# Decoder layer with attention, cross attention and routed experts: 8 of the 79 expert tiles are run between the routing steps of the last sequence, with a ring of 16 results

## The reference, cut to what matters

```python
logits = xf @ Wg.T                       # xf: 4096 tokens, Wg: 16 experts
probs = jax.nn.softmax(logits, axis=-1)
topw, topi = jax.lax.top_k(probs, K)     # K = 2
...
for e in range(E):
    h = jax.nn.silu(xf @ W1[e]) * (xf @ W3[e])
    out = out + gates[:, e:e + 1] * (h @ W2[e])
```

## Time and profile before

| what | value |
| --- | --- |
| time, median of 3 runs | 822.4 us (821.83 to 822.49) |
| the profiled execution, its own time | 823.12 us |
| its span, first to last instruction | 821.3 us |
| granted clock of TensorE, mean | 0.993 of full speed |
| PE busy | 798.6 us, 97% of the span |
| DVE busy | 598.0 us, 73% |
| ACT busy | 432.8 us, 53% |
| POOL busy | 396.8 us, 48% |

### The profile page before, as it was taken

The page is one execution under the profiler, slowest core; times in us unless marked ns, Lnnn a source line. Parts: engine busy times, 40 slices in busy tenths (PEclk is TensorE's granted clock), DMA queues, the critical chain, the costliest instruction groups (busy, mean ns, idle before and its releaser), DMA issues.

```text
span 821.3 us, 21021 instructions
## 1 busy us (share of the span) xinstructions
PE 798.6 (97%) x5949; PEld 758.3 (92%) x5950; DVE 598.0 (73%) x1722; ACT 432.8 (53%) x1185; POOL 396.8 (48%) x567
## 2 busy tenths in 40 slices
PE   9999999999999999999999999999988999999995
PEld 8898999999999999999999999999987799999994
DVE  4757777888787877878787778887675566666663
ACT  4473554637265463737355453726243267667673
POOL 3332134444534454454535444353435358787875
PEclk9999999999999999999999999999999999999997
DMA  8786573655739284564828375573499458777780
GB/s 266 256 290 233 194 256 120 244 204 193 256 125 308 81 281 161 201 242 160 280 95 309 108 254 175 187 263 127 156 425 368 146 106 134 127 132 128 131 132 2
DMA packets 105673, 161.19 MB, mean 196 GB/s; under 512 B 10672, under 2 KB 69616, under 8 KB 104752
## 3 DMA queue, kind: packets, MB, share of 16 engines
q1 hardware_dynamic: 79264, 115.33, 42.0%
q0 software_dynamic: 15792, 35.17, 17.2%
q10 hardware_dynamic: 10576, 10.19, 4.7%
HBM read 50.14 MB, written 112.47 MB: 198 GB/s over the span
## 4 chain that ended last, share of the span: by engine, by line
PE 82%; DVE 6%; ACT 6%; issue 3%; DMA 1%; SPq 1%; POOL 1%; POOLq 0%; DVEq 0%; ACTq 0%
PE ps L797 70%; PE ps L808 5%; PE ps L1037 3%; PE ps L1147 2%; PE ps L1169 2%; ACT fT_hi L1305 2%; ACT relu_v L1306 2%; ACT phi L1292 1%; DVE fT_lo L1508 1%; DVE snmax L1681 1%; DVE smax L1677 1%; DVE pr L1670 1%; DVE xn_attn L1501 0%; ACT pr L1351 0%; DVE stat L1490 0%
## 5 line engine op out<-in xcount | busy, mean ns | idle before, releaser
L788 POOL DMA_INDIRECT out<-narrow,sidx x79 | 122.4, 1549 | 46.1 <-DVE sidx L1886 20.7
L1220 ACT ACTIVATE xn3T<-ps 128x512 f32<-128x512 f32 x17 | 10.2, 597 | 138.8 <-PE ps L808 136.2
L797 PE MATMUL ps<-w_hi,fT_hi 128*128 128x256 f32 x256 | 79.8, 312 | 2.4 <-DVE fT_lo L1508 2.1
L1292 ACT ACTIVATE phi<-ps,nmax 128x128 f32<-128x128 f32 x256 | 73.4, 381 | 9.2 <-DVE nmax L1629 9.0
L1508 DVE TENSOR_TENSOR fT_lo<-relu_v,fT_hi 128x512 fp32r<-128x512 f32 x64 | 52.3, 818 | 33.2 <-ACT relu_v L1306 33.0
L797 PE MATMUL ps<-w_lo,fT_hi 128*128 128x256 f32 x256 | 72.3, 282 | 0.0
L797 PE MATMUL ps<-w_hi,fT_lo 128*128 128x256 f32 x256 | 72.2, 282 | 0.0
L1306 ACT ACTIVATE relu_v<-ps,b_sb 128x256 f32<-128x256 f32 x128 | 69.1, 540 | 0.0
L1305 ACT ACTIVATE fT_hi<-ps,b_sb 128x256 fp32r<-128x256 f32 x128 | 68.0, 531 | 1.5 <-PE ps L797 1.5
L605 POOL TENSOR_TENSOR veps<-mv,eps_ln 128x2 f32<-128x2 f32 x48 | 10.8, 225 | 118.4 <-DVE mv L1494 118.4
L797 PE MATMUL ps<-hT_hi,w_hi 128*128 128x256 f32 x256 | 67.2, 284 | 0.0
(11 more groups left out here) (300 smaller groups left out, 2744.6 us busy)
## 6 DMA issues: line engine op xcount, KB each, us to landing
expert_rows<-zero_rows SPq DMA_DIRECT2D x16, 4352.0 KB, 16.0
narrow<-expert_rows ACTq DMA_DIRECT2D x71, 136.0 KB
expert_up_hi<-X SPq DMA_DIRECT2D x16, 352.0 KB, 2.7
e_lo<-expert_up_lo POOLq DMA_DIRECT2D x2, 2816.0 KB, 12.8
e_hi<-expert_up_hi POOLq DMA_DIRECT2D x2, 2816.0 KB, 22.1
part_raw<-in_E SPq DMA_DIRECT2D x30, 176.0 KB
expert_up_lo<-part_raw SPq DMA_DIRECT2D x15, 352.0 KB, 3.1
X<-in_x SPq DMA_DIRECT2D x16, 256.0 KB
```

The costliest lines, as they stand in the source:

```text
L788: pool.indirect_dma_start(out_rows, bass.IndirectOffsetOnAxis(sidx[:, u:u + 1], 0), yg[:, u, :], None, bounds_check=NT * P - 1, oob_is_err ...
L797: return pe.matmul(out_, lhsT, rhs, start=start, stop=stop)
L1220: return act.activation(out_, in_, ACT.Copy)
L1292: last = act.activation(phi[:, g, h, :], ps[:, g, h * M:(h + 1) * M], ACT.Exp, bias=nmax[:, g, h:h + 1])
```

## The change

- The plan of the first 8 tiles (`EARLY`) is made from the counts of the first 13 sequences (`EARLY_SEQS`): for each expert in turn, its tiles that are already full (`early_count`, `early_sum`, `early_tiles` on DVE, in the last turns). SP loads their rows in the last turn (`load_early`).
- The last turn (`NSEQ + 2`) is gone. The norm, router, choice, count, placing and storing of the last sequence stand between the pieces of slots 0 to 2; the plan of the other tiles (`late_count`, `late_sum`, `late_tiles`) in slots 1 and 2; loading of tiles 8 to 13 in ACT's slot 6 (`load_late`). The filler behind the last cross attention and ahead of the first tile is gone.
- The other tiles leave out what the first 8 took (`taken`).
- `yg` and `sidx` are rings of 16 (`RING`): slot s writes them when scatter s-16 has landed. The rows `xg` stay a ring of 8.
- Scatters among the first 8 tiles wait for the one or two before them whenever the experts differ (`early_waits`), without a test of tokens; tile 8 always waits for tile 7 and 6, tile 9 for tile 7 (the `ALU.max`). From tile 8 the test of meeting tiles is made from both sides. POOL's edge gathers stand behind scatter 1, and the edges are read in slots 9 to 11.
- The expert weights are loaded by SP in pieces, 14 of 16 experts of the low up parts already in turn 15, and `e2a` and `e2b` by POOL at other places of its turn.
- The gate's exponential of the last sequence moves from ACT to POOL, as a power of e.

```diff
+    EARLY = 8
+    RING = 2 * GB
+    EARLY_SEQS = NSEQ - 3
...
+            def early_waits():
+                dve.wait_ge(early_plan, EARLY_TILES)
+                for k in range(1, ADDING):
+                    last = dve.tensor_tensor(other_early[:, k - 1, k:], expert_i[:, k:EARLY], expert_i[:, 0:EARLY - k],
+                                             ALU.not_equal)
+                then(last)
+                for k in range(1, ADDING):
+                    last = dve.scalar_tensor_tensor(added_need[:, k - 1, k:EARLY], other_early[:, k - 1, k:], 16.0,
+                                                    round_of[:, 0:EARLY - k], ALU.mult, ALU.add)
+                last.then_inc(early_plan, 1)
...
+                for k in range(1, ADDING):
+                    last = dve.tensor_tensor(other_expert[:, k - 1, k:], lasts[:, 0:SLOT_TILES - k], firsts[:, k:], ALU.is_ge)
+                then(last)
+                for k in range(1, ADDING):
+                    last = dve.tensor_tensor(meeting[:, k - 1, k:], meeting[:, k - 1, k:], other_expert[:, k - 1, k:],
+                                             ALU.mult)
+                then(last)
+                for k in range(1, ADDING):
+                    last = dve.tensor_scalar(meeting[:, k - 1, EARLY:EARLY + k], meeting[:, k - 1, EARLY:EARLY + k], 1.0, None,
+                                             ALU.max)
...
             def scatter_index(s, u):
-                if not (isinstance(s, int) and s < GB):
-                    hold(dve, scattered[u], (s - u) * PER + 16)
-                dve.tensor_scalar(sidx[:, u:u + 1], xg[:, u, D:D + 1], float(NT * P), None, ALU.add)\
+                if not (isinstance(s, int) and s < RING):
+                    hold(dve, scattered[u % GB], rounds(s, u) - 16)
+                dve.tensor_scalar(sidx[:, u:u + 1], xg[:, u % GB, D:D + 1], float(NT * P), None, ALU.add)\
...
+                if first(s):
+                    place_own(NSEQ - 1, 5)
+                    dve.wait_ge(egap_ready, NSEQ)
+                    gates(NSEQ - 1)
+                if isinstance(s, int) and s == 1:
+                    late_count()
+                    late_sum()
+                if isinstance(s, int) and s == 2:
+                    late_tiles()
...
+            def load_late():
+
+                act.wait_ge(plan_ready, 1)
+                tiles = [tile_of(s) for s in range(EARLY, EARLY + 2)]
+                act.wait_ge(placed, NSEQ * 16 * TOPK * TS)
+                for s in range(EARLY, 2 * EARLY - 2):
+                    load_rows(s, s, tiles[s - EARLY] if s - EARLY < len(tiles) else tile_of(s))
```

More of the change, by code:

```diff
@@ L597, in _ @@
             pool.wait_ge(const_ready, N_CONST - 2)
-            for whole, short in ((before, before_01), (ones, ones_01)):
-                pool.tensor_copy(short[:, :], whole[:, :]).then_inc(const_ready, 1)
+            for whole, short in ((before, before_01), (ones[:, :], ones_01)):
+                pool.tensor_copy(short[:, :], whole).then_inc(const_ready, 1)
             pool.wait_ge(const_ready, N_CONST)
@@ L720, in turn @@
                         split_ctx(b + 1)
-                if r is not None and not last_turn:
+                if r is not None:
                     keep_rows(r)
@@ L1100, in turn @@
                     ffn_out(1, FC - 2, FC).then_inc(w2_ps, 1)
-                if b is not None and not last_ffn:
+                if b is not None and not last_ffn and not last_cross:
                     router(b, 6)
@@ L1283, in turn @@
                     round_part(*splits_of(i))
-                def own_rows(kept):
-                    for j in range(TOPK):
-                        last = copy(kept[:, :, j, 0:D], xn3)
-                    last.then_inc(rows_kept, 1)
                 def features(g):
@@ L1379, in turn @@
                     round_part(splits_of(i)[0])
-                if r is not None and not last_ffn and not last_cross and not last_turn:
+                if r is not None and not last_ffn and not last_cross:
                     choice_counts(r)
@@ L1613, in logits_in, with choice_seen, summed @@
                     .then_inc(logit_ready, 1)
+            def choice_seen(r):
+                hold(dve, chosen, (r + 1) * CHOICE_STEPS)
+                dve.tensor_tensor(oh[:, :, :], hot[:, 0], hot[:, 1], ALU.add).then_inc(oh_ready, 1)
+                if not first(r):
+                    dve.wait_ge(egap_ready, r)
+                dve.tensor_tensor(gap[:, :], best[:, :, 1], best[:, :, 0], ALU.subtract)\
+                    .then_inc(gap_ready, 1)
+            def summed(counted):
+                cum, cbufs, n = counted, (cum_a, cum_b), 1
+                while n < NE:
+                    dst = cbufs[0]
+                    cbufs = cbufs[::-1]
+                    dve.tensor_copy(dst[:, 0:n], cum[:, 0:n])
+                    then(dve.tensor_tensor(dst[:, n:], cum[:, n:], cum[:, 0:NE - n], ALU.add))
+                    cum, n = dst, 2 * n
+                return cum
@@ L1767, in turn @@
                         part_rest(p, n)
-                if b is not None:
+                if b is not None and not last_cross:
                     if not first(b):
```

508 lines of the change are left out of this document (316 added, 192 removed).

## The result

The changed kernel takes 837.12 us (median of 4 runs, 834.24 to 839.49), the kernel before beside it on the same chip 822.44 us: a ratio of 1.0175 (95% interval 1.0141 to 1.0209). It is slower by 14.7 us; the forecast was 832.6, with a range of 825 to 840. The profiled execution has a span of 834.6 us and took 836.78.

A forecast was written before the change was run, and what follows sets the result against it. PE bounds the kernel before, POOL's scatter chain the changed one: start 644.9, plus 58.7, 95.1 and 25.9, puts the last scatter at 824.6; 6.9 more gives a span of 831.5, a median of 832.6 us, range 825 to 840.

The forecast's parts named there:

- Nine neighbour waits, 5.0 us a trip: POOL, scatters 0 to 15: nine wait for the direct neighbour, 5.0 us each; with gathers 58.7 us against 36.5 before.
- Scatter 0 at 644.9: POOL, behind the last sequence's stores: first scatter starts at 644.9 instead of 654.87, 10 us sooner; range 643.5 to 648.
- Weights and early rows, nothing: DMA loads ahead of tile 0: weights arrive in time, early row loads lie under the last cross attention; 0 to 1 us.
- Steps 15 to 64, 95.1 us, and the last 14, 25.9: POOL's later scatters: its own pace as before for 95.1 us, then 14 steps at 1.85 us, 25.9, ending at 824.6.
- The end: After the last scatter: the span ends 6.9 us behind its start at 824.6, giving 831.5 us.
- PE's side, slot 7 at 658.5: PE, first eight slots moved into the 21 us stretch: slot 7 ends near 658.5 instead of 665.5, a 7.0 us gain.
- the faster rival: Short trips let scatters catch PE, whose 7.0 us gain shows: 815.4 us, or up to 822; chance 0.09.
- The ring: The ring of 16 lets PE run ahead but does not make POOL faster; PE loses a us or two near slot 30.
- No change: PE's new waits or half clock in slots 0 to 7 cancel its gain and POOL isn't late: 822.4 us; chance 0.05.

The follow-up runs named there:

- e2: Kernel before with neighbour waits forced at the nine tiles where the changed kernel has them, nothing else changed: 846.72 us, ratio 1.0239.
- e7: Changed kernel with the results of tiles 0 to 14 written nowhere and no waits among those scatters: 828.71 us, ratio 1.0082.
- e0: Changed kernel run again unaltered, on the chip of a later call, for comparison: 837.58 us, ratio 1.020.
- e4: Changed kernel without the 2048 KB load of the low down weights, the high part used instead: 833.07 us, ratio 1.0133.
- e5: Changed kernel with ACT's row loads of tiles 8 to 13 issued two each in slots 5, 6 and 7: 838.24 us, ratio 1.0195.
- e3: Changed kernel with `sidx` waiting for scatter s-8 instead of s-16, `yg` still a ring of 16: 839.06 us, ratio 1.0126.
- e8: Changed kernel with crowded experts first, tiles 8 to 13 loaded in three places, low down weights loaded later, edges tested earlier: 823.95 us, ratio 0.9993.
- e9: The changed kernel with the repairs of e8 but the old order of experts, so nine neighbour waits stay: 836.75 us, ratio 1.014.

## Why the prediction was right, point by point, and what it mis-sized

The direction, the bound and the mechanism came out as forecast. The size is 4.5 us too small: one term is 5.2 too small, and all others together are 0.7 too large.

- **Nine neighbour waits, 5.0 us a trip.** Right in number and place. The nine steps sum to 43.2 us, 4.80 each. Seven of them lie between 4.61 and 4.88, the one at tile 3 takes 5.80, the one at tile 14 3.79. With the gathers, steps 0 to 15 take 57.0 where 58.7 was written: -1.7. e2 shows that the waits alone are enough. One thing the sum leaves out stayed hidden by luck: scatter 8 also waits for the test's numbers, which come in slot 11. By e7 they would hold it to 682.44 without any of the first five waits, 0.9 us before it started.
- **Scatter 0 at 644.9.** This term failed. It starts at 650.07, 5.2 late and 2 beyond the upper bound (648.94 and 4.0 in e0, the same kernel again). The step that went wrong is "Weights and early rows, nothing": the prediction let the loads of the early rows lie under the last cross attention and never asked what else was in the DMA engines when they were issued. They stood behind the down weights `e2b` and `e2a_lo`, landed 6.6 and 9.6 us after their issue where that is known, and left PE idle for 4.3 us and then at 1.2 GHz, ahead of the last sequence's router. The prediction's reading that the DMA engines are full until about 638 was the kernel before's, and it held here until 632. e4 takes 2 MB away and gets scatter 0 at 645.16 and 833.07 us. The low clock itself had been named, but only for the rival in which it cancels the gain.
- **Steps 15 to 64, 95.1 us, and the last 14, 25.9.** Right: 94.9 and 25.9. POOL's 1.85 us set the pace to the end.
- **The end.** 6.7 us behind the last scatter, 6.9 written. +5.2 - 1.7 - 0.2 - 0.2 gives a span of 834.6 for 831.5. The other 1.4 us of the median are what lies around the span (2.2 against 1.8) and that the median is 0.3 above the profiled execution, not 0.7 below.
- **PE's side, slot 7 at 658.5.** Wrong by 10.5 us: it ends at 669.05, 3.5 after the 665.5 of before. The row of small waits had been listed, but not the first hole, nor that ACT issues six loads (4.96 us in the timeline) before it splits tile 8's rows, nor the half clock in both. The second hole did not reach the time, since PE isn't the bound there (e5); the first did, through scatter 0. Had the waits been cheap, all of it would have counted: e7 is the faster rival put to the test, and it takes 828.7, not 815.4.
- **The ring.** That it only lets PE run on is right within 2.5 us (e3).
- **The rivals.** "Faster" needed trips of 3.9 us. One of nine was shorter. The rule weighed there, of the Trainium skill ("DMA: Bandwidth & Descriptors", section "Anatomy of one DMA — SWDGE (gpsimd) path"), gives an estimate of 2.3 us for a transfer of this size; the landing of L844 is 2.7, 3.9 and 4.5, so the trace doesn't agree. "No change" had the half clock on PE right and POOL wrong.

So the loss has two layers. POOL's chain is the outer one, and by e7 8.9 us can be had by taking its waits away. Then PE is the bound, 5.2 us late at its last result. Of the two holes the first is worth more: by tile 71's result from the mark, its repair brings PE 4.7 to 5.4 us (e4 against e0 and the changed kernel), that of the second 2.9 to 3.6 (e5), and with both e8 is 3.7 ahead of the kernel before, for 7.0 forecast at slot 7.

## What to carry to other kernels

An engine that sits off the bound at 1.85 us of 2.00 has no room: count the waits that a new order puts into its chain before counting what the new order saves elsewhere. A wait costs only what it takes beyond the next wait of the same instructions: five of the nine here cost 0.9 us together, four cost nearly 11. When work is moved ahead of a stretch that was idle, look at what the DMA engines carry at that time; here small loads that the moved work needs were issued beside megabytes that are needed only later. And after one such wait is taken out, look for the next at the same place: here the late rows and the late test hid behind the nine waits, at nearly the same scatter.

## What the runs showed of the hardware that was not expected

- Row loads of 136 KB of the hardware queue landed late beside a load of 2048 KB of POOL's queue that was still under way (617.1 to 629.6): the third after 9.56 us, the sixth after 6.63. With that load held back, the first landed after 4.40 and the third after 4.56 (e9). While both queues had work, at 622 to 628, POOL's took 91.4% of the DMA engines' time and the other 12.7%.
- After 6 us in which PE was busy 0.48, 0.00 and 0.79 of 2 us each (626 to 632) the clock was 0.50 for 6 us, although PE was then busy 1.80, 2.00 and 2.00 of 2; the same after the hole at 658.
- A dependent scatter's trip is no constant: 3.79 to 5.80 us in one kernel, up to 6.47 in another with the same nine waits (e9). The same kernel run again differs by 0.7 us over its 15 steps (57.7 in e0, 57.0), e9 by 2.6. The trips over ACT's six row loads are the long ones, as said at e9.
